# Expert output biases summed on DVE from the third tile on, instead of products on PE, with new order tables

## The reference, cut to what matters

```
combined = [norm(x), attention over the context, anchor]              # 3 * 256
router_probs = softmax(combined @ router_W + router_b)                # 3 experts
h = silu(combined @ e_w1 + e_b1)                                      # 3 * 512
expert_out = h @ e_w2 + e_b2
routed = sum over e of expert_out[e] * router_probs[e]
x = x + sigmoid(silu(combined @ gate_w1 + gate_b1) @ gate_w2 + gate_b2) * (routed @ out_w + out_b)
```

## Time and profile before

| what | us |
|---|---|
| median of three runs | 457.73 |
| the three runs | 455.22, 457.79, 457.73 |
| profiled execution, its own time | 453.57 |
| profiled execution, span from first to last instruction | 451.8 |
| PE busy in the span | 428.3 |
| DVE busy in the span | 287.6 |
| ACT, POOL busy | 220.2, 167.8 |

### The profile page before, as it was taken

The page is one execution under the profiler, slowest core; times in us unless marked ns, Lnnn a source line. Parts: engine busy times, 40 slices in busy tenths (PEclk is TensorE's granted clock), DMA queues, the critical chain, the costliest instruction groups (busy, mean ns, idle before and its releaser), DMA issues.

```text
span 451.8 us, 9521 instructions
## 1 busy us (share of the span) xinstructions
PE 428.3 (95%) x3606; PEld 388.4 (86%) x3606; DVE 287.6 (64%) x720; ACT 220.2 (49%) x485; POOL 167.8 (37%) x177
## 2 busy tenths in 40 slices
PE   8889999979999999999999999999999999989794
PEld 7558899979999999999999889899989999867564
DVE  5768536484584399438863795389539844965835
ACT  2785634226337543663466346634663465335161
POOL 6555455552453155124432552245224232211000
PEclk9999899999999999999999999999999999999598
DMA  7659010640300220213000300120011002002000
GB/s 283 243 192 352 2 48 18 159 93 1 72 3 4 52 66 4 72 39 103 1 28 15 82 1 28 28 68 1 28 33 40 3 27 52 20 27 53 21 26 23
DMA packets 15569, 27.21 MB, mean 60 GB/s; under 512 B 3006, under 2 KB 7838, under 8 KB 15396
## 3 DMA queue, kind: packets, MB, share of 16 engines
q1 hardware_dynamic: 15232, 26.19, 19.3%
q10 hardware_dynamic: 292, 0.41, 0.4%
HBM read 15.94 MB, written 2.10 MB: 40 GB/s over the span
## 4 chain that ended last, share of the span: by engine, by line
PE 68%; DVE 19%; ACT 5%; issue 3%; SPq 3%; DMA 1%; POOL 0%; DVEq 0%; ACTq 0%
PE hidden_banks L1580 6%; PE hidden_banks L1582 6%; PE hidden_banks L1581 6%; PE score_banks L1926 5%; DVE head_maxima L1381 5%; PE token_bank L1580 4%; PE score_banks L1587 4%; PE token_bank L1581 4%; PE token_bank L1582 4%; PE value_bank L1942 3%; PE score_banks L1901 3%; PE value_bank L1945 3%; PE hidden_banks L1794 2%; PE head_bank L1587 2%; SPq L793 2%
## 5 line engine op out<-in xcount | busy, mean ns | idle before, releaser
L1512 POOL TENSOR_TENSOR hidden_low<-hidden,hidden_high 128x512 fp32r<-128x512 f32 x56 | 72.2, 1289 | 128.5 <-ACT hidden_high L995 128.1
L995 ACT CAST hidden_high<-hidden 128x512 fp32r<-128x512 f32 x56 | 34.8, 621 | 62.0 <-DVE hidden L1320 60.9
L1061 ACT ACTIVATE exp_ring<-score_banks 128x512 f32<-128x512 f32 x96 | 52.0, 605 | 26.0 <-PE score_banks L1926 26.0
L1580 PE MATMUL hidden_banks<-normed_high,hidden_w_high 128*128 128x256 f32 x224 | 64.3, 287 | 0.0
L1381 DVE TENSOR_REDUCE head_maxima<-score_banks 128x2 f32<-128x308 f32 x128 | 53.9, 469 | 14.4 <-PE score_banks L1901 14.3
L1581 PE MATMUL hidden_banks<-normed_high,hidden_w_low 128*128 128x256 f32 x224 | 62.7, 280 | 0.0
L1582 PE MATMUL hidden_banks<-normed_low,hidden_w_high 128*128 128x256 f32 x224 | 62.6, 280 | 0.0
L1320 DVE SCALAR_TENSOR_TENSOR hidden<-hidden,hidden_banks 128x512 f32<-128x512 f32 x56 | 38.1, 681 | 37.8 <-ACT hidden L987 37.2
L1580 PE MATMUL token_bank<-expert_out_high,hidden_high 128*128 128x256 f32 x192 | 55.7, 290 | 0.0
L1581 PE MATMUL token_bank<-expert_out_high,hidden_low 128*128 128x256 f32 x192 | 53.6, 279 | 0.0
L1582 PE MATMUL token_bank<-expert_out_low,hidden_high 128*128 128x256 f32 x192 | 53.4, 278 | 0.0
(11 more groups left out here) (262 smaller groups left out, 1121.7 us busy)
## 6 DMA issues: line engine op xcount, KB each, us to landing
unit_weights<-units SPq DMA_DIRECT2D x7, 768.0 KB, 4.8
query_stack<-queries_high SPq DMA_DIRECT2D x56, 64.0 KB, 2.0
tokens<-x SPq DMA_DIRECT2D x8, 256.0 KB, 3.5
query_stack<-queries_low SPq DMA_DIRECT2D x28, 64.0 KB, 2.0
w_slice<-units SPq DMA_DIRECT2D x7, 256.0 KB, 2.9
out<-tokens SPq DMA_DIRECT2D x7, 256.0 KB, 2.2
w_T<-folds SPq DMA_DIRECT2D x6, 256.0 KB, 5.4
pair_keys<-keys_high SPq DMA_DIRECT2D x16, 77.0 KB
```

The costliest lines, as they stand in the source:

```text
L995: nc.scalar.copy(SH[:, ring(t, u), :], TB[:, ring(t, u), :]).then_inc(scalar_h, 1)
L1061: nc.scalar.activation(E[:, w % ERING, :], S[:, ring_of[key][0], :], ACT.Exp).then_inc(scalar_score, 1)
L1512: nc.gpsimd.tensor_tensor(SL[:, ring(t, u), :], TB[:, ring(t, u), :], raw(SH[:, ring(t, u), :]), ALU.subtract).then_inc(gpsimd_h, 1)
L1580: mm(out_, lh, rh, start=start, stop=False, skip_group_check=skip)
```

## The change

For tiles 0 and 1 nothing changes in what is computed where. For tiles 2 to 7 (`t >= PLAIN`) the products with `second_bias` behind u = 2, 4 and 6 are left out. A new DVE step `init` (t) writes `expert_sum` first: for expert 0 the bias row times the probability, for experts 1 and 2 multiplied and added, each for the two halves of the tile, six instructions of 128x256. `evac` of j = 1 then adds to it. A new step `bias2` in tile 1 spreads the three bias rows over all partitions: three PE products into `value_bank` and two ACT copies. The bias arrays lie where `value_bias_row` and `second_bias_columns` lay. All order tables have new numbers; of those the diff shows a few rows.

```diff
@@ constants
+PLAIN = 2
...
@@ tables (a few rows)
-    "unit": (0.96, 2.05, 3.29, 4.46, 8.07, 9.82, 10.57), "w2": (7.46, 10.42, 12.34, 13.87, 15.19, 17.85),
+    "vt": (0.65, 1.84, 2.91, 3.19, 4.54, 7.26, 9.2), "unit": (-0.2, 1.3, 3, 3.4, 7.9, 9.1, 10.4),
...
@@ schedule()
+    for i in range(2):
+        place(SETUP["bias2"][i], ("bias2", i))
...
+        if t >= PLAIN:
+            place(at + plan(t, "init"), ("init", t))
...
@@ memory
+        BX = put("expert_bias", [P, 2, D], offset=bias_at)
+        BX3 = put("expert_bias3", [P, D], offset=columns_at)
...
@@ ACT
+            def expert_bias(key):
+                i = key[1]
+                act.wait_ge(tensor_bias2, upto(tensor_bias2, key, "m"))
+                if i:
+                    nc.scalar.copy(BX3[:, :], V0[:, 0:D]).then_inc(scalar_bias2, 1)
+                    return
+                act.wait_ge(keys_placed[1], 16 * (3 * GROUPS + 1))
+                act.wait_ge(vector_key, upto(vector_key, ("key", 1), "vt"))
+                nc.scalar.copy(BX[:, :, :], halves(V0[:, :])).then_inc(scalar_bias2, 1)
...
@@ DVE
+            def init(key):
+
+                t = key[1]
+                dve.wait_ge(scalar_bias2, upto(scalar_bias2, ("bias2", 1), "b"))
+                dve.wait_ge(vector_logit, upto(vector_logit, ("logit", t), "prob"))
+                dve.wait_ge(vector_res, upto(vector_res, ("res", t - 1), "x"))
+                for e in range(EXPERTS):
+                    if e:
+                        dve.wait_ge(vector_results, results.n)
+                    for s in range(NSUB):
+                        p, bias = PR[:, t % 2, s, e:e + 1], BX[:, e, :] if e < 2 else BX3[:, :]
+                        if e == 0:
+                            last = v.tensor_scalar(ACC[:, s, :], bias, p, None, ALU.mult)
+                        else:
+                            last = v.scalar_tensor_tensor(out=ACC[:, s, :], in0=bias, scalar=p, in1=ACC[:, s, :],
+                                                          op0=ALU.mult, op1=ALU.add)
+                    if e < EXPERTS - 1:
+                        last.then_inc(vector_results, results.one())
+                last.then_inc(vector_init, 1)
+
             def evac(key):
                 t, j = key[1:]
                 dve.wait_ge(tensor_p, upto(tensor_p, ("p", t, 2 * j), "p"))
-                if j == 1:
+                if j == 1 and t >= PLAIN:
+                    dve.wait_ge(vector_init, upto(vector_init, ("init", t), "b"))
+                elif j == 1:
                     dve.wait_ge(vector_logit, upto(vector_logit, ("logit", t), "prob"))
...
-                    if j == 1:
+                    if j == 1 and t < PLAIN:
                         last = v.tensor_scalar(ACC[:, s, :], bank, p, None, ALU.mult)
...
@@ PE
+            def expert_bias(key):
+                i = key[1]
+                if i:
+                    pe.wait_ge(scalar_bias2, upto(scalar_bias2, ("bias2", 0), "b"))
+                else:
+                    pe.wait_ge(vector_w2, upto(vector_w2, ("w2", NU - 1), "l"))
+                for j in range(2 - i):
+                    e = 1 + 2 * i + j
+                    last = mm(V0[:, D * j:D * j + D], BSEL[:, e:e + 1].to_broadcast([P, P]), CB[:, :], start=True, stop=True)
+                last.then_inc(tensor_bias2, 1)
...
-                        last = exact(bank, (SH[:, ring(t, u), c], SL[:, ring(t, u), c]), (wh, wl), first, False, skip=True)
-                        if u % 2 == 0 and i == 1:
+                        last = exact(bank, (SH[:, ring(t, u), c], SL[:, ring(t, u), c]), (wh, wl), first, t >= PLAIN and u > 0 and u % 2 == 0 and i == 1, skip=True)
+                        if u % 2 == 0 and i == 1 and (t < PLAIN or u == 0):
                             last = mm(bank, BSEL[:, j:j + 1].to_broadcast([P, P]), CB[:, :], start=False, stop=True, skip_group_check=True)
```

More of the change, by code:

```diff
@@ L208 @@
         "z": ["s"],
+        "init": ["b"],
         "evac": ["o"],
@@ L242 @@
     "tensor": {
-        "norm": 1.2, "qx": 0.9, "prob": 1.2, "keyx": 2,
+        "norm": 1.6, "qx": 0.96, "prob": 1, "keyx": 1.75,
     },
     "scalar": {
-        "cv": 0.1, "ck": 0.3, "fold": 0.3, "vw": 0.2, "vt": 0.4, "w2": 0.4, "keyx": 2.3, "norm": 1.4, "att": 0.4,
-        "logit": 0.5, "z": 0.44, "h": 0.4, "gate": 0.1, "qx": 1.1, "query": 0.2, "row": -0.6, "score": 0.01,
-        "out": 1.3, "stack": 3.5,
+        "cv": 0.2, "ck": 0.1, "fold": -0.4, "vw": 0.4, "vt": 0.5, "w2": 0.6, "keyx": 2.2, "norm": 1.7, "att": 0.7,
+        "logit": 0.8, "z": 0.4, "h": 0.43, "gate": 0.17, "qx": 0.9, "query": 0.1, "row": -0.6, "score": 0.12,
+        "out": 2.3, "stack": 1.2,
     },
     "vector": {
-        "fold": -0.57, "vw": 0.7, "vt": 0.5, "w2": 0.9, "att": 0.1, "route": 0.1, "logit": 1.1, "z": 0.8,
-        "evac": 0.5, "query": 0.8, "most": 0.44, "row": 0.3, "proj": 0.6, "last": -4.1, "key": 1.1, "mod": -0.3,
-        "bq": 0.4, "cb": 0.3,
+        "fold": 0.6, "vw": 0.75, "vt": 0.64, "w2": 1.2, "att": 0.4, "route": 0.1, "logit": 1.2, "z": 0.7,
+        "evac": 0.7, "query": -0.1, "most": 0.31, "row": 0.4, "proj": 0.7, "last": -3.5, "key": 1.1, "mod": -0.4,
+        "bq": 1.5, "cb": 0.6,
     },
     "gpsimd": {
-        "h": 0.5, "ln": 0.8, "qn": 0.75, "low": 1.1, "keyn": 2.4, "split": -0,
+        "h": 0.7, "ln": 0.8, "qn": 0.7, "low": 1.6, "keyn": 3.1, "split": 1.2,
     },
     "sync": {
-        "query": 16.3, "row": -2.7, "proj": -4.1, "last": -11.3, "key": -7.2, "place": 17.3,
+        "query": 13.6, "row": -1, "proj": -2.5, "last": -14.4, "key": -10.6, "place": 22.5,
     },
@@ L268 @@
 PLAN = {
[L269 to L276 removed]
+    "init": 6.3, "dup": (36.6, 41.2), "za": -0.3, "step": 1.99, "z": 0.5, "h": 0.96, "p": 3.19, "again": 3,
+    "vw": -30, "ln": -0.4, "norm": 1.3, "low": 7.7, "att": 7.73, "prob": 8.99, "route": 12.4, "logit": 13.3,
+    "res": 16.3, "qn": 16.8, "shift": 18.1, "xhat": 18.8, "qx": 18.3, "qlow": 20.2, "query": 20.46,
+    "most": (22.24, 22.69, 23.42, 25.38, 25.92, 27.07, 27.41, 28.17), "row": (28.76, 46.01),
+    "stack": (18.7, 18.7, 19.5, 26.8),
+    "score": (31.25, 31.28, 31.65, 32.79, 32.8, 32.98, 34.03, 34.04, 34.12, 34.7, 35.04, 35.72),
+    "value": (33.3, 33.6, 36, 36.1), "raw": (33.8, 36.6), "sum": (32.2, 36.7), "sums": (37.3, 58), "out": (39, 40.8),
+    "outl": (42.6, 80.1), "proj": 45, "last": (39.5, 64.8), "reload": 67.7,
 }
@@ L1437, in _ @@
                      "vw": context_w, "vt": context_tail, "w2": w2, "cb": bias_out, "mod": mod, "bq": query_bias, "keyn": keyn, "key": pair_keys, "ln": ln,
[L1438 removed]
+                     "att": att, "prob": prob, "route": route, "logit": logit, "z": hidden, "init": init, "evac": evac,
                      "res": res, "qn": qn, "shift": shift, "qlow": qlow, "query": query, "most": most, "row": row, "dup": dup, "outl": outs_low, "sums": sums,
```

79 lines of the change are left out of this document (42 added, 37 removed).

## The result

| what | before | changed |
|---|---|---|
| median of 20 runs each, us | 455.27 (452.10 to 458.07) | 452.37 (450.43 to 456.40) |
| ratio, 95% interval | 1 | 0.9941 (0.9918 to 0.9964) |
| profiled execution: own time, span | 453.57, 451.8 | 453.33, 451.3 |

The change makes the kernel 0.6% faster, 2.7 us: more than no difference, less than 1%. The two profiled executions are only 0.2 us apart, since before's is among its faster runs and the changed one's is 1 us over its median. The pair must therefore be read by stages, not by its ends.

What follows compares the result with a forecast made beforehand. PE was taken to bound the kernel, except in the maxima, paced by DVE, and parts of the setup. Terms -2.55 + 0.35 + 0 + 2.0 - 1.7 - 0.9 - 0.4 = -3.2 us gave 454.5 us, range 449.8 to 459.5.

Steps and rivals of the forecast that it cites:

- 0.35 of `bias2`: Tile 1: three added PE products at 0.116 us each, +0.35 us, with +0.5 as the upper end.
- Products removed, -2.55: Tiles 2 to 7: of 36 bias products taken from PE, 22 count, -2.55 us; bounds 0 and -4.2.
- The tables inside the tiles, 0: All tiles: no cost counted for the new order, since DVE's order of the tiles is nearly what it was.
- rival D: Maxima of each tile: the tables add a wait of 1 us a tile, +6 us, 460.5; chance 0.07.
- `init`, 0: DVE between qlow and query, six tiles: 2.1 to 2.8 us hidden in a 3.35 us wait for ACT, no cost.
- Rival C: DVE before query: init not covered because a POOL instruction falls on it, 458.9, or 471 if DVE bound throughout; chance 0.06.
- The start, +2.0: Setup: ACT takes unit 0 first and waits for its transfer, first hidden unit 1 to 2 us late; ends 0 and +4.7.
- Rival A: Setup: the start costs nothing, since PE waits there anyway; -5.7 us, 452.0; chance 0.23.
- rival B: Head of ACT's queue: late fold moves the whole setup 3.0 us and brings a half-clock period, +1.6, 459.3; chance 0.14.
- `mod` steps, -1.7: Setup, 50 to 60 us: spreading 32 narrow PE products avoids the clock's fall behind them, -1.7 us; ends -1.7 and 0.
- p(0, 5), -0.9: Router of tile 1: this step ahead of logit fills PE's wait, -0.9 us; ends -1.4 and 0.
- The end, -0.4: Last eight PE products: four fill steps right ahead may keep the clock, -0.4 us, range 0 to -0.9.

Runs made afterwards that it cites:

- bias change alone: The kernel before with its own tables, given the bias change (init directly behind qlow, bias2 in tile 1): ratio 0.9962 (0.9927 to 0.9996).
- the tables alone: The changed kernel with PLAIN = 8, so all bias products stay on PE and no init runs: ratio to the kernel before 0.9987 (0.9961 to 1.0014).

## Why the prediction held, and where it did not

The gain was forecast as 3.2 us and measured as 2.7. The forecast of 454.5 us stood on a median of three runs, 457.73; of 20 runs it is 455.27, and 452.4 for the changed kernel lies in the range of 449.8 to 459.5. By stages of the profiled pair: first hidden unit +0.8 (forecast +2.0); from there to the first `row` -2.6 (forecast -1.7 - 0.9 + 0.35, of which no run isolates the 0.35 of `bias2`); from there to `row` of tile 6 -1.7 (forecast about -2.5); from there to the first `row` of tile 7 +3.1 (no term); behind it 0.0 (forecast -0.4). The pair's spans differ by 0.5, the medians by 2.7, so that the 2.7 lies near the 3.2 is in part luck: a loss that had no term, and a pair of executions in which the start was cheap.

- *Products removed, -2.55*: right in mechanism and size. 0.46 us a tile was forecast; the distance fell by 0.37 (bias change alone) and 0.50 (against the tables alone), u = 6 counts and u = 4 doesn't, but for the one distance above.
- *The tables inside the tiles, 0*: wrong. They cost 0.27 us a tile, so the changed kernel's distance is only 0.23 us shorter than before (0.40 and 0.45 from tile 2 to 4, 0.14 from 4 to 5, and from 5 to 6 it is 0.17 longer). That is rival D's effect at a quarter of its size; which steps in the table do it is open.
- *`init`, 0*: right in what it costs the kernel, wrong in its reason. Undisturbed it takes 2.44 us (bias change alone), between the 2.1 and 2.8 forecast. I had written that "nothing meets it". That came from POOL's times in the kernel before; the new order brings POOL's `sum` under `init`, and the collision makes it 3.85 us. The gap had grown too, from 3.35 to 3.85 + 0.73 = 4.58 us; under the old gap `init` would have stuck out by 0.5 us, so this is luck. Rival C's condition occurred in five of six tiles, without its price, and the doubled `init` shows that even 1.65 us over the cover cost next to nothing in the middle tiles.
- *POOL against DVE*: the same instruction takes 482 ns on average where POOL is idle and up to 1404 ns where it runs, 1.4 us a tile. The rule of the Trainium skill ("SBUF — State Buffer", section "SBUF: two separate sides"), by which DVE with two SBUF inputs and GpSimd lock each other out, agrees with these rows.
- *The start, +2.0*: the size is right on average, the make-up is not. The first hidden unit came 0.8 us late in this pair, 0.8 to 3.1 in the eight executions with the wait, 2.0 on average. `vt` was 2.5 us late where 3.0 was forecast, but not for the forecast reason: the transfer landed at 9.39, so `fold` began 0.25 us late instead of 2.1. With a landing as late as I had put it (11.47, the tables alone) `vt` is 4.5 us late. What comes back is more than I said: the other edits in the setup tables bring the first hidden unit 2.3 us forward, and ACT's wait takes 3.1 or more from it. As a price of its own the wait is about 1% of the kernel (0.9941 against 0.9838), of the 1.6% that the rest of the change wins. Rival A, that it is free, is refuted; rival B's mechanism, the late `vt`, is in every execution, and its condition (over 3 us at the first hidden unit) was met in one of eight. I had not seen that this one wait costs more than the whole change is left with.
- *`mod` steps, -1.7*: the clock behaved as said. With the -0.9 of p(0, 5) the forecast for this stretch fits the pair (-2.6); undone by itself in the changed kernel, their place is worth 5.5 us, with the order of DVE in it.
- *p(0, 5), -0.9*: 1.9 in one profile, 0.9 by the ratios, not resolved.
- *The end, -0.4*: the last eight products ran at 1.00 instead of 0.55, and from the start of these products to the end it took 3.85 us instead of 4.64: -0.8. But these products also start 0.7 us later after `row` of tile 7, and from there to the end the two kernels take the same 28.3 us, so nothing was won.
- *Not in the prediction*: the wait before the scores of tile 6 and the fall of the clock behind it, +3.1 us in the pair of profiles, 2.3 of it the clock. I had looked at PE's removed work in tile 7 only as a gain, and had not asked what the new order does to PE's waits behind tile 6, where it is the tables that make the wait, and the removed products only lengthen it from 1.42 to 1.66 us.

Open: what in the tables lengthens the tiles, why the same order of instructions has a fall of the clock in one execution and none in the next, and the division of the `mod` price.

## What to carry to other kernels

Work taken from a busy engine counts only in the stretches that it paces; measure the distance between equal steps of two tiles, not busy time. A wait for a transfer at the head of a queue is paid by everybody behind it, here with 1% of the kernel, so a step that waits goes behind the copies that others wait for; and undo each moved step by itself, since one bad number in a good table stays hidden in the sum. Where work in front of a wait goes away or moves, so that short waits join into a long one, look at the clock behind it.

## What the runs showed of the hardware

- One wait of PE of 1.66 to 1.67 us was followed by 3.4 to 6.8 us at the lower clock in five executions and by none in a sixth with the same order there; at 1.42 us in the same place it was not in either of two. Executions of one kernel differ by 3 to 8 us (the kernel before with unit 0 first: 457.4 us at a mean granted clock of 0.969, 463.6 at 0.959), more than most of the edits are worth.
- The same transfer of unit 0, issued at 3.1 to 3.8 us, was there between 9.4 and 11.5 us in nine executions in which an engine waited for it.
- Two instructions that collide on DVE and POOL both pay: POOL's `hidden_low` took 1.48 us instead of 1.28, DVE's 1.40 instead of 0.47.
